# A decoder layer on one core: feed-forward weights loaded during the cross attention, covariance from centred rows, first similarities in halves

## What is computed

```python
q = jnp.einsum('bnd,de->bne', x, w_q)                       # 2048 columns: 16 blocks of 128
mean = jnp.mean(q, axis=(0, 1))
var = jnp.var(q, axis=(0, 1))
q = (q - mean) * jax.lax.rsqrt(var + BN_EPS) * bn_gamma + bn_beta
q = q.reshape(b, n, 2, H, KD).transpose(2, 0, 1, 3, 4)
sim = jnp.einsum('pbnhd,hkpd->pbnhk', q, keys)              # 2 x 8 heads x 32 keys a token
sx, ix = jax.lax.top_k(sim[0], TOPK)
sy, iy = jax.lax.top_k(sim[1], TOPK)
...                                                         # best 8 of 64 sums: experts of 1024
h = gelu_new(jnp.einsum('bnd,bnhkd->bnhk', x, down_embed[indices]))
h = jax.nn.softmax(scores, axis=-1) * h
out = jnp.einsum('bnhk,bnhkd->bnd', h, up_embed[indices])
```

## Time and profile before

| | us |
|---|---|
| median of three runs | 1376.27 |
| the three runs | 1375.0, 1376.27, 1378.77 |
| the profiled execution | 1373.3 |
| its span | 1371.5 |
| of the span busy: PE, PEld | 1176.9, 923.8 |
| DVE, ACT, POOL | 1116.3, 849.1, 618.9 |

### The profile page before, as it was taken

The page is one execution under the profiler, slowest core; times in us unless marked ns, Lnnn a source line. Parts: engine busy times, 40 slices in busy tenths (PEclk is TensorE's granted clock), DMA queues, the critical chain, the costliest instruction groups (busy, mean ns, idle before and its releaser), DMA issues. The chain is left out here.

```text
span 1371.5 us, 32769 instructions
## 1 busy us (share of the span) xinstructions
PE 1176.9 (86%) x13174; PEld 923.8 (67%) x13174; DVE 1116.3 (81%) x2700; ACT 849.1 (62%) x994; POOL 618.9 (45%) x445
## 2 busy tenths in 40 slices
PE   3567999998999999999999999999997547777788
PEld 2454677776777767777776777677775526776678
DVE  5886888887889888897888888888885278999984
ACT  0347778877778786777778778887773531222121
POOL 2254856566475666656476575667230000000000
PEclk9768999999999999999999999999998665666656
DMA  7016999999999999999999999999997200000000
GB/s 150 1 38 131 193 199 198 190 196 194 195 188 197 195 191 197 196 189 192 201 195 194 194 193 196 191 190 190 188 190 139 69 1 1 5 5 5 5 5 6
DMA packets 695185, 191.77 MB, mean 140 GB/s; under 512 B 681045, under 2 KB 692601, under 8 KB 694905
## 3 DMA queue, kind: packets, MB, share of 16 engines
q1 hardware_dynamic: 695032, 189.67, 81.5%
HBM read 18.92 MB, written 0.82 MB: 14 GB/s over the span
## 5 line engine op out<-in xcount | busy, mean ns | idle before, releaser
L1003 PE MATMUL ps<-pT,xa_hi 128*128 128x128 f16 (+1 forms) x2496 | 415.9, 217 | 27.2 <-DMA pT<-p 26.9
L999 PE MATMUL ps<-pT,xa_hi 128*128 128x128 f16 (+1 forms) x2496 | 417.5, 217 | 21.4 <-ACT uT L840 20.1
L823 ACT ACTIVATE e<-ps,bias 128x1444 f32<-128x1444 f32 (+1 forms) x208 | 305.4, 1468 | 194.4 <-DVE bias L889 194.1
L887 DVE TENSOR_REDUCE nmax<-ps 128x1 f32<-128x1444 f32 (+1 forms) x208 | 344.5, 1656 | 95.3 <-PE ps L985 94.2
L1000 PE MATMUL ps<-pT,xa_lo 128*128 128x128 f16 (+1 forms) x2496 | 417.6, 217 | 0.0
L831 ACT ACTIVATE p<-e 128x1444 f16<-128x1444 f32 (+1 forms) x208 | 294.5, 1416 | 8.5 <-DMA pT<-p 0.5
L896 DVE TENSOR_TENSOR p<-e,p 128x1444 f16<-128x1444 f32 x144 | 268.1, 1862 | 11.4 <-ACT p L831 7.8
L999 PEld LDWEIGHTS ps<-pT,xa_hi 128*128 128x128 f16 x2496 | 242.8, 98 | 49.4 <-issue 33.6
L785 POOL TENSOR_TENSOR p<-e,p 128x1444 f16<-128x1444 f32 x64 | 187.5, 2930 | 180.3 <-ACT p L831 178.4
L1003 PEld LDWEIGHTS ps<-pT,xa_hi 128*128 128x128 f16 x2496 | 242.7, 98 | 34.1 <-DMA pT<-p 33.8
L1000 PEld LDWEIGHTS ps<-pT,xa_lo 128*128 128x128 f16 x2496 | 242.7, 98 | 13.1
(11 more groups left out here) (219 smaller groups left out, 1794.9 us busy)
## 6 DMA issues: line engine op xcount, KB each, us to landing
raw<-in_ctx SPq DMA_DIRECT2D x16, 704.0 KB
pT<-p SPq DMA_TRANSPOSE x416, 4.5
f_wq<-in_L_ffn_w_q SPq DMA_DIRECT2D x1, 1024.0 KB, 4.9
f_wqt<-in_ffn_wq_t SPq DMA_DIRECT2D x2, 512.0 KB, 7.0
x_tok<-in_x SPq DMA_DIRECT2D x1, 800.0 KB
out_x<-ost SPq DMA_DIRECT2D x6, 128.0 KB, 1.8
wk_t<-in_wk_t SPq DMA_DIRECT2D x1, 512.0 KB, 5.9
wq_t<-in_wq_t SPq DMA_DIRECT2D x1, 512.0 KB, 8.2
```

Source lines behind the costliest of these rows:

```text
L823: act.activation(e32[t % E_BUF][rows, :], score_banks(t)[rows, 0:T], ACT.Exp, bias=bias[rows, t % N_BUF:t % N_BUF + 1]).then_inc(e_done, 1)
L887: dve.tensor_reduce(nmax[rows, k:k + 1], score_banks(t)[rows, 0:T], AX_X, ALU.max, negate=True).then_inc(max_done, 1)
L999: pe.matmul(out, hi, ph, start=n == 0, stop=False)
L1003: last = pe.matmul(out, hi, pl, start=False, stop=n == NTILE - 1)
```

## The change

It has five parts.
- The feed-forward weights lie in buffers that exist from the start (FfnWeights); the first stage uses the same memory for three of its own arrays. Eight loads at the start of ffn() are replaced by 15 between the transposes of cross(): slots (13, i), (14, i) and (15, i) with i = 1, 4, 7, 10, of which (15, 10) is empty. One semaphore counts the eleven that the set-up needs, another the four expert halves.
- GpSimd adds the rows of x2 into x2sum, one batch behind, in slot (b, 7). The mean comes from two matmuls with ones; VectorE centres the rows themselves (xc), and the covariance is made from them. Of x2T only the first group of 400 tokens is turned before the similarities.
- The covariance is now the stationary side and w_q the moving one: four matmuls of 512 columns. The sum over features, which VectorE made, becomes sixteen matmuls with a column of ones. Three operations that bound the variance become one.
- sim_w and the similarities of step 0 are made and copied in halves of 256 columns, and VectorE's maxima of step 0 follow by halves.
- The tables iota_c and iota_j and a half of iota_w are widened by GpSimd, the other half of iota_w by ScalarE, behind the copies of step 0.

```diff
-        xr = sb("xr", [S, B, D])
-        x2b = sb("x2b", [S, B, D])
...
         rot_a = sb("rot_a", [D, G, S])
...
+                if (b, i) in WEIGHT_SLOTS:
+                    load_weights(sp, m["weights"], a, WEIGHT_SLOTS[b, i])
...
+                if i == 7 and 0 < b < B:
+                    pool.wait_ge(y_norm, 4 * b)
+                    pool.wait_ge(x2sum_done, b)
+                    pool.tensor_tensor(out=m["x2sum"][:, :], in0=m["x2sum"][:, :], in1=x2[:, b - 1, :], op=ALU.add).then_inc(x2sum_done, 1)
...
+class FfnWeights:
+
...
+        experts = sb("f_experts", [P, 2, NE])
+        self.down, self.up = experts[:, 0, :], experts[:, 1, :].rearrange("e (c d) -> e c d", d=D)
+        self.setup_ld, self.expert_ld = sem("setup_ld"), sem("expert_ld")
+        self.buffers = (self.wqt[0:S, :, :], self.wq[0:S, :].rearrange("s (b d) -> s b d", d=D),
+                        experts[0:S, :, :].rearrange("s a (b d) -> s (a b) d", d=D))
...
+SETUP_LOADS, EXPERT_LOADS = 11, 4
+WEIGHT_SLOTS = {(b, i): 4 * n + k for n, b in enumerate(range(B - 3, B)) for k, i in enumerate((1, 4, 7, 10))}
...
+def load_weights(sp, f, a, k):
+
+    if k < 4:
+        e = slice(k * 4 * KD, (k + 1) * 4 * KD)
+        sp.dma_start(f.wq[:, e], a["L0_ffn_w_q"][:, e]).then_inc(f.setup_ld, 16)
+    elif k < 8:
+        n = slice(4 * (k - 4), 4 * (k - 3))
+        sp.dma_start(f.wqt[:, n, :], a["ffn_wq_t"][n.start * KD:n.stop * KD, :].rearrange("(n e) d -> e n d", e=KD)).then_inc(f.setup_ld, 16)
+    elif k == 8:
+        sp.dma_start(f.keys[:, :, :], a["ffn_keys_t"].rearrange("e s h k -> e (s h) k")).then_inc(f.setup_ld, 16)
+        sp.dma_start(f.gam[:, :], a["L0_ffn_bn_gamma"]).then_inc(f.setup_ld, 16)
+        sp.dma_start(f.bet[:, :], a["L0_ffn_bn_beta"]).then_inc(f.setup_ld, 16)
+    elif k == 9:
+        for e in range(0, NE, NE // 2):
+            sp.dma_start(f.down[:, e:e + NE // 2], a["ffn_down_t"][:, e:e + NE // 2]).then_inc(f.expert_ld, 16)
+    elif k == 10:
+        up = a["L0_ffn_up_embed"].rearrange("(c e) d -> e c d", e=P)
+        for c in range(0, NE // P, 4):
+            sp.dma_start(f.up[:, c:c + 4, :], up[:, c:c + 4, :]).then_inc(f.expert_ld, 16)
...
         def _(sp):
-            for dst, src in ((f_wq[:, :], a["L0_ffn_w_q"]),
-                             (f_wqt[:, 0:FH, :], a["ffn_wq_t"][0:FH * KD, :].rearrange("(n e) d -> e n d", e=KD)),
...
-                             (f_up[:, :, :], a["L0_ffn_up_embed"].rearrange("(c e) d -> e c d", e=P))):
-                sp.dma_start(dst, src).then_inc(f_ld, 16)
...
+            pool.wait_ge(fc_done, 6)
+            pool.tensor_copy(iota_c[:, :, :], iota_f[:, 0:2 * NC].rearrange("p (e a) -> p e a", a=1).to_broadcast([P, 2 * NC, P]))
+            pool.tensor_copy(iota_j[:, :, :], iota_f[:, 0:K8].rearrange("p (j a) -> p j a", a=1).to_broadcast([P, K8, K8])).then_inc(narrow_done, 1)
+            def wide_rows(k):
+                es = slice(k * P // 4, (k + 1) * P // 4)
+                pool.tensor_copy(iota_w[:, es, :], iota_f[:, es].rearrange("p (e a) -> p e a", a=1).to_broadcast([P, P // 4, P])).then_inc(wide_pool, 1)
...
+            wide_rows(0)
+            pool.wait_ge(var_done, 1)
...
                 combine(i)
+                if i == 0:
+                    wide_rows(1)
...
         def _(act):
-            for k in range(NG):
+            def turned_out(k):
...
+                act.activation(x2T[:, group(k)], ps[:, 7, 0:G * S], ACT.Copy).then_inc(x2T_done, 1)
...
             act.activation(sim_c[0:1, :], ps[0:1, 6, :], ACT.Copy).then_inc(simc_hi, 1)
-            for k in range(NG):
...
-                act.activation(xct[:, k * G:(k + 1) * G, :], ps[0:S, 4 + k % 2, :].rearrange("s (b d) -> s b d", b=G), ACT.Copy).then_inc(xct_done, 1)
+            turned_out(0)
             act.wait_ge(cov_ps, 1)
...
-            act.activation(iota_w[:, :, :], iota_f[:, :].rearrange("p (e a) -> p e a", a=1).to_broadcast([P, P, P]), ACT.Copy)
-            act.activation(iota_c[:, :, :], iota_f[:, 0:2 * NC].rearrange("p (e a) -> p e a", a=1).to_broadcast([P, 2 * NC, P]), ACT.Copy)
...
-            act.wait_ge(simw_ps, 1)
-            act.activation(sim_w[:, :], ps[:, 5, :], ACT.Copy).then_inc(simw_done, 1)
+            for p in range(2):
+                act.wait_ge(simw_ps, p + 1)
+                act.activation(sim_w[:, sim_half(p)], ps[:, 4 + p, 0:HALF_SIM], ACT.Copy).then_inc(simw_done, 1)
+            for p in range(2):
...
+                ins = act.activation(simb[:, :, p * FH:(p + 1) * FH, :].rearrange("s a n k -> s a (n k)"),
+                                     ps[:, 2 * p:2 * p + 2, 0:HALF_SIM], ACT.Copy)
+                ins.then_inc(first_done, 1)
+            for k in range(1, NG):
+                turned_out(k)
+            act.activation(iota_w[:, P // 2:P, :], iota_f[:, P // 2:P].rearrange("p (e a) -> p e a", a=1).to_broadcast([P, P // 2, P]), ACT.Copy).then_inc(wide_done, 1)
...
-            sims_out(0)
...
-            dve.wait_ge(x2T_done, NG)
-            dve.tensor_reduce(mean[:, :], msum[:, :], AX_X, ALU.add).then_inc(mean_done, 1)
+            dve.tensor_tensor(out=total[:, :], in0=x2sum[:, :], in1=x2[:, B - 1, :], op=ALU.add).then_inc(total_done, 1)
+            dve.wait_ge(mean_ps, 1)
+            for k in range(NG):
+                ks = slice(k * G, (k + 1) * G)
+                dve.scalar_tensor_tensor(out=xc[:, ks, :], in0=ps[0:S, 3, 0:D].rearrange("s (a d) -> s a d", a=1).to_broadcast([S, G, D]),
+                                         scalar=-1.0 / NT, in1=x2[:, ks, :], op0=ALU.mult, op1=ALU.add).then_inc(xc_done, 1)
+            dve.tensor_scalar(mean[:, :], ps[:, 3, D:D + 1], 1.0 / NT, None, ALU.mult).then_inc(mean_done, 1)
...
-            for k in range(NG):
-                ks = slice(k * G * S, (k + 1) * G * S)
-                dve.tensor_scalar(xcT[:, ks], x2T[:, ks], mean[:, 0:1], None, ALU.subtract).then_inc(xcT_done, 1)
...
+                dve.tensor_scalar(xcT[:, group(k)], x2T[:, group(k)], mean[:, 0:1], None, ALU.subtract).then_inc(xcT_done, 1)
...
+            centred(0)
...
-                ns = slice(4 * k, 4 * k + 4)
+                es = slice(k * 4 * KD, (k + 1) * 4 * KD)
...
-                dve.tensor_tensor(out=cw[:, ns, :], in0=ps[:, 1 + k, :].rearrange("e (n d) -> e n d", n=4),
...
-                ins = dve.tensor_reduce(var[:, ns], cw[:, ns, :], AX_X, ALU.add)
...
+                dve.tensor_tensor(out=cw[:, es], in0=ps[:, k % 3, :], in1=f_wq[:, es], op=ALU.mult).then_inc(cw_done, 1)
...
+            dve.tensor_scalar(var[:, :], ps[:, 6, 0:NB], 0.0, EPS, ALU.max, ALU.add).then_inc(var_done, 1)
...
-            dve.wait_ge(wide_done, 1)
...
+                else:
+                    for part in range(2):
+                        dve.wait_ge(first_done, part + 1)
+                        dve.sem_inc(f_waited, 1)
+                        for hf in range(nh):
+                            for n in range(part * FH, (part + 1) * FH):
+                                ins = dve.max(top[0:w, hf, n, :], simb[0:w, hf, n, :])
...
+                if i == 0:
+                    for k in range(1, NG):
+                        centred(k)
+                    dve.wait_ge(narrow_done, 1)
...
+                if i == 0:
+                    dve.wait_ge(wide_done, 1)
+                    dve.wait_ge(wide_pool, 2)
...
-            pe.wait_ge(f_ld, 16 * 8)
+
+            pe.wait_ge(f.setup_ld, 16 * SETUP_LOADS)
...
-            for k in range(NG):
-                pe.wait_ge(xcT_done, k + 1)
...
-                    b = k * G + j
-                    last = pe.transpose(ps[0:S, 4 + k % 2, j * D:(j + 1) * D], xcT[:, b * S:(b + 1) * S], ident[:, :])
...
+            pe.wait_ge(ones_done, 2)
+            pe.wait_ge(total_done, 1)
+            pe.matmul(ps[0:S, 3, 0:D], ones_s[:, :], total[:, :], start=True, stop=True)
+            pe.matmul(ps[:, 3, D:D + 1], total[:, :], ones_s[:, 0:1], start=True, stop=True).then_inc(mean_ps, 1)
+            turn(0)
...
-                    pe.wait_ge(xct_done, b // G + 1)
-                last = pe.matmul(ps[:, 0, 0:D], xct[:, b, :], xct[:, b, :], start=b == 0, stop=b == B - 1)
+                    pe.wait_ge(xc_done, b // G + 1)
+                last = pe.matmul(ps[:, 0, 0:D], xc[:, b, :], xc[:, b, :], start=b == 0, stop=b == B - 1)
...
+            for k in range(4):
+                if k == 3:
+                    pe.wait_ge(cw_done, 1)
+                pe.matmul(ps[:, k % 3, :], cov[:, :], f_wq[:, k * 4 * KD:(k + 1) * 4 * KD], start=True, stop=True).then_inc(cw_ps, 1)
+            pe.wait_ge(simc_rest, 4)
...
-                last = pe.matmul(ps[:, 1 + n // 4, (n % 4) * D:(n % 4 + 1) * D], f_wq[:, n * KD:(n + 1) * KD], cov[:, :], start=True, stop=True)
...
+                if n % 4 == 0:
+                    pe.wait_ge(cw_done, n // 4 + 1)
+                last = pe.matmul(ps[:, 6, n:n + 1], cw[:, n * KD:(n + 1) * KD], ones_d[:, :], start=True, stop=True)
...
-            for n in range(NB):
```

(63 more changed lines are left out.)

83 lines of the change are left out of this document (38 added, 45 removed).

## The result

The kernel before took 1376.36 us in these runs (median of 4), the changed one 1384.57 (median of 4): ratio 1.0058, 95% interval [1.0035, 1.008], **8 us slower**, and 1.1 us beyond the end of the range.

What follows compares the result with a forecast made beforehand. The prediction took the cross attention's sync DMA queue to be as full as TensorE, and ScalarE's run to end the set-up. Loads +9 and set-up -8 gave +1 on 1376.3: 1377.3 us, range 1369.5 to 1383.5.

Steps and rivals of the forecast that it cites:

- The loads, +9: Sync queue, last three cross attention batches: 0.9 us per 256 KB piece, less gaps and slack, adds 9 us.
- Their places: Cross attention: batches 13 and 14 would take 59 to 60 us, batch 15 be longer by 3 to 4.
- The issue alone, 0.40 us: Sync queue: lower price of a load; 15 x 0.40 = 6.0, less 2.9 of gaps, 3.1 us.
- rival 1: Cross attention: loads ride along at issue cost, +3.1, with -7.9 kept: -5 us, 1371; chance 0.30.
- The set-up, -7.9: Feed-forward start: without the load wait, step 0's softmax sum comes at 1112.3 instead of 1120.2, 7.9 us earlier.
- The end of it: Set-up's end: VectorE could reach the softmax sum at 1106.3 but waits for ScalarE's exponent until 1112.3.
- the covariance: Feed-forward set-up: half of its 16 matmuls counted at the half clock, done at 1067.6.
- the variance matmuls: Feed-forward set-up: sixteen matmuls replacing VectorE's four sums, priced like the covariance stage at 3.7 us.
- The second witness: Cross attention: batches with a 722 KB context load take 2.3 us more, so 3.4 MB would add 10.9 us.
- the queue is as full as TensorE: Sync queue, cross attention: transposes stand back to back, so added transfers lengthen the end, less 2.9 us of gaps.
- Rival 2: Cross attention: queue full to the end, 1.1 us a piece, +12.2 - 7.9 = +4.3, up to +7: 1381; chance 0.18.
- Rival 3: Feed-forward set-up: GpSimd's casts at 2.3 ns an element hold up VectorE, +5 us on the sum, 1382; chance 0.12.

Runs made afterwards that it cites:

- experiment 3: The changed kernel with all its loads issued at the start of the cross attention, the slots empty: 1372.12 us, ratio 0.9985.
- experiment 4: The kernel of experiment 3 with fifteen loads of 8 KB, into a table nobody reads, in the fifteen slots: 1379.15 us, ratio 1.0029.
- 9: The kernel before with only its buffers changed, as in 7, plus 384 unused bytes a partition behind the weights' tables: 1375.81 us, ratio 1.0014.
- 12: kernel 10 with 384 unused bytes a partition, p and pT at the old place within 512 bytes: 1358.51 us, ratio 0.9906.
- 7: The kernel before with only its buffers changed, loads still at the start of the feed-forward stage, in fifteen pieces: 1379.48 us, ratio 1.0049.
- 8: The kernel before with one unused table of 128 bytes a partition ahead of the cross attention's tables, no instruction different: 1381.12 us, ratio 1.0057.
- kernel 10: The kernel of experiment 3 with ScalarE's half of iota_w and turning of token groups 1 to 3 moved into ScalarE's wait: 1366.71 us, ratio 0.9942.
- 11: kernel 10 with 224 unused bytes a partition, so p and pT start at a multiple of 512 bytes: 1329.57 us, ratio 0.9681.
- experiment 13: The changed kernel, loads in slots, with 224 unused bytes a partition, p and pT at a multiple of 512 bytes: 1335.91 us, ratio 0.9735.
- experiment 14: The kernel before with 352 unused bytes a partition, p and pT at a multiple of 512 bytes, no instruction different: 1341.76 us, ratio 0.9779.
- 15: kernel 10 with 32 unused bytes a partition, p and pT at 320 within 512 bytes: 1359.69 us, ratio 0.9916.
- kernel 17: kernel 10 with p at a multiple of 512 bytes and pT at 288 within 512: 1327.95 us, ratio 0.9678.

## Why the prediction was wrong

The sum was +9 for the loads, -7.9 for the set-up, +1 in all; measured were +8.

- **The loads, +9: right, 10 us measured** (experiment 3). Their places were less well told: batch 14 at 61.3 us and 9.5 us more behind the start of batch 15 are above the 59 to 60 and the 3 to 4 that the prediction looked for, batch 13 at 57.4 is below. "The issue alone, 0.40 us" was too low an end: in a full queue 8 KB took 0.88 in the median (experiment 4), twice the row from which I took it. So rival 1 was never on. (The four gaps of the old queue add up to 3.0 us, not 2.9, which moves nothing.)
- **The set-up, -7.9: 6.8 measured.** The end of it was right (ScalarE's run binds, the exponent releases the sum). Too short were the covariance, counted at 5.4 us and 6.76 long since the clock stayed at half, and the variance matmuls, 3.7 against 4.57, also partly at half.
- **The failed step is one that isn't in the sum: where the tables lie.** I counted the new buffers at nothing, without a word. They move p from 160 to 32 within 256 bytes and cost 5 to 8 us (5 in experiments 9 and 12, 5 to 7 in 7, 8 in 8). +10 - 6.8 + 5 = +8.2 is the measured loss, but 5 is the low end: with 8 it would be 3 more, and each of the three terms is known to a few microseconds only, so that the sum closes is no proof. The changed kernel with its loads in the slots and p back at 160 within 256, which would show this term in the change itself, was not run; what was run is the same step in the kernel before (8) and in kernel 10 (12).
- **The second witness was a false one.** I read 59.05 against 56.75 us a batch as the price of a context load. With p aligned, the same loads cost nothing, 56.9 us with and without (experiments 11, 13 and 14). The rows were right, and so was "the queue is as full as TensorE"; the cause I gave for it was not: the queue was full because each transpose took 0.3 us longer than it needed to, its source lying off a multiple of 256 bytes already in the kernel before (experiment 14: 30 us with no instruction changed).
- **Rival 2** ("the queue is full to the end") names what happened in batches 14 and 15, at +12.2 and up to +7 in sum; the loads cost 10, and its point, 1.1 us a piece, wasn't reached. **Rival 3** is false: about 0.9 ns an element, done at 1087.3, 12 us before the power.
- In the prediction I called the Trainium skill contradicted by the trace. Its page "DMA: Bandwidth & Descriptors", section "Rules for kernel authors", says of a DMA issued early only that the fixed setup cost overlaps; that the load is then free was my reading. Even that reading comes out to about 1 us where the queue has room (experiment 13). The trace spoke against it because the queue was full.

What stays open: why 32 within 256 bytes is worse than 64 or 160. The runs show that it is (experiments 8, 9, 12, 15), not how: the engines' packet time isn't the longest there, and the sums of the 416 transposes' times in the queue overlap (825 to 829 us over the kernels at 32, 823 at 64, 821 to 827 at 160). That the second transaction is what makes a piece slower off a multiple of 256 is the page's account; it fits the table and the tenth more of packet time, but no trace shows a transaction.

## What to carry to other kernels

A new or longer table is an edit of every table behind it. Where DMA transposes are near the bound, write down where their source starts before and after the change, and pad it to a multiple of 256 bytes; an unused pad in the old kernel shows in one run whether places matter. And before pricing an added transfer by what others seem to cost in a full queue, ask why it is full: a queue with room took these loads for about 1 us instead of 10.

## What the runs showed of the hardware

- DMA transposes of 128 x 1536 halves (12 pieces of 256 bytes a row) held the queue for 1.81 us each in the median with the source at 160 within 512 bytes (kernel before), and for 1.52 with it at a multiple of 256 (experiment 13); both are second halves. The end, over 416 of them, was 1372.2 against 1341.8 us in the kernel before, unpadded and aligned, on one chip (experiment 14). The share of time in which the 16 DMA engines held packets of that queue fell with it, in the kernel before and then in kernel 17:

```profile
q1 hardware_dynamic: 695032, 189.67, 81.5%
```

```profile
q1 hardware_dynamic: 695656, 189.67, 75.2%
```

- Fifteen loads of 8 KB between transposes in a full queue held it for 0.88 us each in the median, 0.43 to 0.96 (experiment 4); the two in experiment 13, where there was room, for 0.45 and 0.33. The changed kernel's two, in the full queue, took 0.44 and 0.89.
- TensorE's clock rose 5 to 6 us after work resumed in the kernel before, and 9 to 10 us after in the changed one, with other work in between: the covariance took 3.58 us there, at the full clock, and 6.76 here, mostly at half.
